# Attention inside a four-block model: a group's maxima turned and their score unit issued ahead of the step's end, score units moved up by one place, query chunks moved

## The reference, cut to what matters

```python
q = (x @ wq_w.T + wq_b).reshape(b, t, H, HD)          # H = 32, HD = 32
k = (x @ wk_w.T + wk_b).reshape(b, t, HKV, HD)        # HKV = 1
v = (x @ wv_w.T + wv_b).reshape(b, t, HKV, HD)
scores = jnp.einsum('bqhd,bkd->bhqk', q, k1) / jnp.sqrt(jnp.float32(HD))
scores = jnp.where(causal, scores, -jnp.inf)
weights = jax.nn.softmax(scores, axis=-1)
attn = jnp.einsum('bhqk,bkd->bqhd', weights, v1)
return attn.reshape(b, t, H * HD) @ wo_w.T + wo_b
```

## Time and profile before

| | |
|---|---|
| median of 3 runs | 2989.56 us (2985.69 to 2994.57) |
| the profiled execution's own time | 2977.39 us |
| its span, first to last instruction | 2975.7 us |
| PE busy | 2750.2 us (92%) |
| DVE, ACT, POOL busy | 1679.5, 1159.2, 948.6 us |
| mean granted TensorE clock | 0.958 |

### The profile page before, as it was taken

One profiled execution on the slowest core, in us unless ns is written; L12 is line 12 of the kernel. 1 busy time (PEld: TensorE's weight loads), 2 busy tenths in 40 slices (PEclk: granted clock), 3 DMA queues, 4 the chain that ended last, 5 costly groups with the idle time before them and its releaser, 6 DMA issues. The chain is left out here.

```text
span 2975.7 us, 41796 instructions
## 1 busy us (share of the span) xinstructions
PE 2750.2 (92%) x15104; PEld 2015.2 (68%) x15104; DVE 1679.5 (56%) x4305; ACT 1159.2 (39%) x2509; POOL 948.6 (32%) x1460
## 2 busy tenths in 40 slices
PE   5888999999999999999999987999999999999988
PEld 3556667667566676676665565777877777878766
DVE  3554464663745646637445346666666666666653
ACT  3664464562644645626445012222222222222220
POOL 2433122221221222212213044444444444444422
PEclk8889999999999999999999888999999999999989
DMA  5755545444536454445455510010101010102011
GB/s 157 197 167 157 167 104 163 124 113 145 129 82 174 109 154 125 113 144 124 94 143 153 172 43 1 4 54 3 55 4 54 5 54 2 56 1 57 2 27 29
DMA packets 103631, 272.29 MB, mean 92 GB/s; under 512 B 12122, under 2 KB 23514, under 8 KB 101122
## 3 DMA queue, kind: packets, MB, share of 16 engines
q1 hardware_dynamic: 102706, 269.55, 33.6%
q10 hardware_dynamic: 720, 0.07, 0.0%
HBM read 168.40 MB, written 50.33 MB: 74 GB/s over the span
## 5 line engine op out<-in xcount | busy, mean ns | idle before, releaser
L664 DVE CUSTOM_DVE_ANT_0 ps_attn<-ps_attn,later_keys 128x512 f32<-128x512 f32 (+3 forms) x1024 | 485.9, 512 | 403.0 <-PE ps_attn L837 400.7
L474 POOL TENSOR_SCALAR_AFFINE_SELECT pt<-pt 128x512 f32<-128x512 f32 x256 | 165.4, 648 | 905.1 <-ACT pt L561 903.9
L561 ACT ACTIVATE pt<-ps_attn 128x512 f32<-128x512 f32 (+1 forms) x704 | 385.9, 560 | 102.1 <-PE ps_attn L865 90.4
L1559 PE MATMUL ps_mixer<-m_w_hi,m_xt_hi 128*128 128x512 f32 x1024 | 421.2, 411 | 1.6 <-DVE m_xt_lo L1341 1.6
L576 ACT ACTIVATE ps_attn<-ps_attn,top 128x512 f32<-128x512 f32 (+1 forms) x512 | 312.6, 611 | 247.1 <-DVE top L664 245.1
L1560 PE MATMUL ps_mixer<-m_w_hi,m_xt_lo 128*128 128x512 f32 x1024 | 406.4, 397 | 0.0
L1561 PE MATMUL ps_mixer<-m_w_lo,m_xt_hi 128*128 128x512 f32 x1024 | 405.8, 396 | 0.0
L865 PE MATMUL ps_attn<-q_stack,k_stack 97*128 97x512 f32 (+3 forms) x1024 | 314.4, 360 | 37.2 <-DMA q_stack<-top_rows 25.7
L837 PE MATMUL ps_attn<-k_stack,q_stack 96*128 96x512 f32 (+3 forms) x1024 | 306.6, 352 | 38.6 <-DMA q_stack<-q_lo 15.0
L1241 ACT CAST m_xt_hi<-ps_mixer 128x512 fp32r<-128x512 f32 x192 | 104.1, 589 | 494.0 <-PE ps_mixer L1554 493.8
L837 PEld LDWEIGHTS ps_attn<-k_stack,q_stack 96*128 96x128 f32 x1024 | 175.5, 195 | 129.1 <-ACT ps_attn L576 72.8
(11 more groups left out here) (216 smaller groups left out, 4937.0 us busy)
## 6 DMA issues: line engine op xcount, KB each, us to landing
xr<-in_a_x SPq DMA_DIRECT2D x64, 512.0 KB, 6.8
q_stack<-q_hi SPq DMA_DIRECT2D x128, 256.0 KB, 5.6
wq_hi<-wq_split SPq DMA_DIRECT2D x56, 512.0 KB, 3.9
wq_lo<-wq_split SPq DMA_DIRECT2D x56, 512.0 KB, 4.6
q_stack<-q_lo SPq DMA_DIRECT2D x64, 256.0 KB, 6.8
wo_hi<-wo_split SPq DMA_DIRECT2D x8, 2048.0 KB, 8.3
wo_lo<-wo_split SPq DMA_DIRECT2D x8, 2048.0 KB, 13.1
x<-xr SPq DMA_DIRECT2D x32, 512.0 KB, 2.8
```

The lines of the kernel that those rows point to most:

```text
L561: nc.scalar.activation(pt[k][:, heads[0]:heads[0] + len(heads), :].rearrange("p j t -> p (j t)"), ps[:, ST0 + n % 2, 0:width * len(heads)] ...
L664: mm = nc.vector.tensor_tensor_reduce(part, part, later_keys[:, T - width:T], 1.0, NO_SCORE, ALU.add, ALU.min, top[:, j * TILES + i:j * TI ...
L1559: nc.tensor.matmul(out, a_hi, b_hi, start=first, stop=False)
```

## The change

Four things are moved; no instruction is added to or taken from the work that a group needs.

1. The turn, `copy_rows` and `shift` of group M+1 come in step M where `turned_early(M + 1)` holds, which is for all groups but the last two of each sequence (groups 6 and 7; those of the last sequence are early too). On PE the turn stands ahead of turned unit 10 of group M, on ACT the copy ahead of `exps` 10, on SP the DMA at the end of step M, ahead of the stores of an output run. Before, all three stood at the start of step M+1.
2. Score units move up: units 2 and 3 behind turned unit 0, and from there unit u+3 behind turned unit u, where unit u+2 stood. `weigh_first` stands behind score unit 1, before it stood ahead of score unit 0.
3. The query chunks of a step with projection were spread as 0 ahead of the turn, 1 and 2 behind score units 0 and 1, then 3, (4, 5), (6, 7) behind turned units 0, 1, 2; now chunk 0 stands behind score unit 0, then (1, 2), (3, 4), (5, 6, 7) behind turned units 0, 1, 2.
4. In step 6 `q_high` moves from u = 2 to u = 4 on ACT, and `q_low` behind `tops` 7 on DVE. In the other steps both stay.

Two waits for PSUM banks (`y_added` in `tops_turned`, `top_rows_done` in `output`) are set one group later to fit.

```diff
--- before.py
+++ after.py
@@ -335,6 +335,9 @@
         def x_banks(b, t):
             return (AV, DEN) if b == 0 and t % 2 else (PROJ, MISC)
 
+        def turned_early(G):
+            return inside(G) and not (G % GROUPS >= GROUPS - 2 and G // GROUPS + 1 < BATCH)
+
         def wq_group(M):
             return M + 3 if M + 3 < GROUPS else None
 
@@ -430,7 +433,7 @@
                     if M == NG:
                         sp.wait_ge(b_done, 2 * NG)
                         early.load(sp)
-                    if inside(M):
+                    if inside(M) and not turned_early(M):
                         shift(M)
                     if M > GROUPS and M % GROUPS == 1 and inside(M):
                         load_wo(M // GROUPS - 1)
@@ -458,6 +461,8 @@
                         store_wo_chunk(c)
                     if (c := wo_chunk(M + 1)) is not None:
                         load_wo_chunk(c)
+                    if turned_early(M + 1):
+                        shift(M + 1)
                     if (run := output_run(M)) is not None:
                         b, r = run
                         store(b, 2 * r)
@@ -623,11 +628,13 @@
                     if M == -1:
                         q_high(1)
                     for u in range(U):
+                        if u == U - 1 and turned_early(M + 1):
+                            copy_rows(M + 1)
                         if inside(M):
                             exps(M, (u,))
                         if inside(M + 1):
                             row_sum(M + 1, u + 2)
-                        if u == 2 and inside(M + 2) and M != -1:
+                        if u == (4 if second is not None else 2) and inside(M + 2) and M != -1:
                             q_high(M + 2)
                         if u == 3 and M == -1:
                             wq_high(act, 2)
@@ -732,10 +739,12 @@
                         normalise(dve, b, t)
                     if inside(M + 1):
                         tops(M + 1, (4, 5))
-                    if inside(M + 2) and M != -1:
+                    if second is None and inside(M + 2) and M != -1:
                         q_low(M + 2)
                     if inside(M + 1):
                         tops(M + 1, (6, 7))
+                    if second is not None and inside(M + 2):
+                        q_low(M + 2)
                     if inside(M - 1):
                         invert(M - 1, 0)
                     if inside(M + 1):
@@ -849,8 +858,8 @@
                         pe.wait_ge(v_done, b + 2)
                     if G:
                         pe.wait_ge(top_rows_done, G)
-                    if b and g in (1, 2):
-                        pe.wait_ge(y_added, Y_TILES * (b - 1) + TILES * g)
+                    if b and g in (2, 3):
+                        pe.wait_ge(y_added, Y_TILES * (b - 1) + TILES * (g - 1))
                     nc.tensor.transpose(ps[:, MISC, 0:P], top[:, :].bitcast(F32), ident_f).then_inc(topt_ready, 1)
 
                 def turned_scores(G, u):
@@ -911,7 +920,7 @@
                         elif t == 0:
                             pe.wait_ge(qlo_done, min(GROUPS * (b + 1) + run + 3, NG))
                         else:
-                            pe.wait_ge(top_rows_done, min(GROUPS * (b + 1) + run + 1, NG))
+                            pe.wait_ge(top_rows_done, min(GROUPS * (b + 1) + run + 2, NG))
                         tok = slice(t * P, (t + 1) * P)
                         for c in range(CH):
                             if run == 0 and t == 0 and c == CH - 1:
@@ -923,30 +932,33 @@
                 for M in STEPS:
                     first, second = coming(M, 5), coming(M, 6)
                     project = second is None and inside(M + 2)
-                    shares = ((0, 1, 2, 3, 4), (5, 6), (7,), (), (), ()) if M == -1 else ((0,), (1,), (2,), (3,), (4, 5), (6, 7))
+                    shares = ((0, 1, 2, 3, 4), (5, 6), (7,), (), (), ()) if M == -1 else ((), (0,), (), (1, 2), (3, 4), (5, 6, 7))
                     if project:
                         q_part(M + 2, shares[0])
-                    if inside(M):
+                    if inside(M) and not turned_early(M):
                         tops_turned(M)
                     if second is not None:
                         transposes(second, 2)
-                    if inside(M - 1):
-                        weigh_first(M - 1)
                     if inside(M + 1):
                         scores(M + 1, 0)
                     if project:
                         q_part(M + 2, shares[1])
                     if inside(M + 1):
                         scores(M + 1, 1)
+                    if inside(M - 1):
+                        weigh_first(M - 1)
                     if project:
                         q_part(M + 2, shares[2])
                     if second is not None:
                         transposes(second, 3)
                     for u in range(U):
+                        if u == U - 1 and turned_early(M + 1):
+                            tops_turned(M + 1)
                         if inside(M):
                             turned_scores(M, u)
-                        if u + 2 < U and inside(M + 1):
-                            scores(M + 1, u + 2)
+                        if inside(M + 1):
+                            for n in ((2, 3), (4,), (5,), (6,), (7,), (8,), (9,), (10,))[u] if u < 8 else ():
+                                scores(M + 1, n)
                         if project and u < 3:
                             q_part(M + 2, shares[u + 3])
                         if second is not None:
```

## The result

| | before | after |
|---|---|---|
| median of 4 runs | 2987.62 us | 3078.01 us (3066.07 to 3083.47) |
| the profiled execution's own time, span | 2977.39, 2975.7 | 3080.04, 3078.3 |
| mean granted TensorE clock | 0.958 | 0.935 |

The changed kernel is slower: ratio 1.0324, 95% interval 1.0296 to 1.0352. The direction is the forecast one, but the step is +90 us where +43 was forecast, and the time lies just outside the range. The fourth run of before, made beside the changed kernel, brings its median from 2989.56 to 2987.62; the quotient of the two medians is 1.0303, inside the interval.

The account below looks back on a forecast made before the run. An ordinary step was taken as bounded by TensorE and DVE at once. Six batches +28, the last +5, the first +5, shift waits -5 and clock +10 made +43 on 2989.56: 3033 us, range 2982 to 3075.

Parts of the forecast that it names:

- A: Ordinary step, from the turn to the last query matmul: grows from 8.30 to 9.66 us.
- B: Ordinary step, from the last query matmul to the next turn: shrinks from 8.28 to 7.93 us, limited by DVE.
- "faster" rival: Ordinary steps: the turn comes as early as TensorE's own work allows, steps about 16 us, total 2945; chance 0.14.
- The stack's landing: Ordinary step: the query stack's DMAs land 9.2 us behind the last query matmul.
- a wait of 0.6: TensorE at score unit 0: reaches it at 8.6 us and waits 0.6 us for the stack, making the period 18.2.
- The table: Forecast times by step M % 8: 39.5 for output runs, 18.2 for ordinary steps, 19.9, 28.6 and 18.4 for steps 5 to 7.
- +4.7 a batch from the chains: Over a batch of eight steps: time grows from 195.8 to 200.5 us.
- the forecast without its clock term: Whole kernel: the forecast growth of +43 us without the 10 us added for the clock.
- The clock, +10 in all: Whole kernel: TensorE idles twice around each turn, for which 10 us were added.
- the clock falls more often: TensorE around early turns: a clock fall in every one of 50 steps, +65 us instead of 10, 3088; chance 0.13.
- every second one: The case of a clock fall in every second step, priced at 3055 us in all.
- Shift waits, -5: TensorE's waits for the shift, 4.5 us in 1400: cured by the earlier copy and shift, counted as -5 us.

Follow-up runs that it names:

- l1: The changed kernel with q_low written behind maxima 7 in every step: 3091.4 us, ratio 1.0386 to the kernel before.
- u3: The changed kernel with the query chunks placed as in the kernel before: 3041.3 us, ratio 1.0223 to the kernel before.
- f4: The changed kernel with four unread matmuls ahead of each early turn, its wait for DVE behind them: 3027.5 us, ratio 1.0183 to the kernel before.
- f2: The changed kernel with two unread matmuls ahead of each early turn, its wait for DVE behind them: 3063.0 us, ratio 1.0289 to the kernel before.
- f7: The kernel before with the early turn alone and seven unread matmuls ahead of each early turn: 3001.6 us, ratio 1.0070 to the kernel before.
- f6: The changed kernel with four unread matmuls ahead of each early turn and two more ahead of score unit 0: 3032.8 us, ratio 1.0198 to the kernel before.
- p1: The kernel before with the early turn, copy and shift alone: 3089.1 us, ratio 1.0393 to the kernel before.
- p3: The kernel before with the query chunks moved back alone: 3087.6 us, ratio 1.0375 to the kernel before.

## Why the prediction was right or wrong

- **A, turn to last query matmul, 9.66:** right, 9.8: 10.49 less 0.66 of stack wait.
- **B, last query matmul to turn, 7.93:** right, 7.81, and maxima 7 at 2.70 as forecast (2.7). But the reason that I gave the "faster" rival, q_low in the way, is wrong: l1 shows that row sum 5 and score unit 7 hold maxima 7.
- **The stack's landing, 9.2, and a wait of 0.6 where a step's score unit 0 needs it:** right, 1251.85 - 1242.53 = 9.32 to the start of score unit 0, a wait of 0.65 to 0.78. That 0.6 less would come out without it is wrong: u3 is free of the wait and has the same 18.31.
- **The table:** 39.38 for 39.5, 18.29 for 18.2. Step 6 fell to 30.1, not 28.6. Alone, part 4 did a little better than I said, 28.9 on average where the sum without the chunk's move gives 29.2. In the whole change a new wait of 2.54 takes its place, that of score unit 4 for row sum 2. Row sum 2 waits 1.03 on ACT for maxima 2; these stand on DVE behind the low part of the transposed tokens, which waits 1.54 for ACT's casts:

```profile
859.64 1.29 DVE L658 TENSOR_TENSOR xn_lo<-ps_attn,xn_hi 128x512 fp32r<-128x512 f32 x2 [1.54 <-ACT xn_hi L545]
861.63 0.66 ACT L581 ACTIVATE ps_attn<-ps_attn,top 128x512 f32<-128x512 f32 x1 [1.03 <-DVE top L671]
862.46 0.44 PE L846 MATMUL ps_attn<-k_stack,q_stack 96*128 96x384 f32 x1 [2.54 <-ACT ps_attn L581]
```

- **+4.7 a batch from the chains:** right in size. f4, whose low time is nearly that of before, has 1013.1 - 984.2 = 28.9 in five batches; less 7 us of low clock at 0.46, 25.7, that is 5.1 a batch. In part that is luck: in f4's two batches whose only fall is that of step 6, step 5 takes 21.1 to 21.2 where I had 19.9, step 7 takes 17.0 where I had 18.4, and the two cancel. Over all of attention, to the last turn, f4 is 1654.8 - 1611.6 = 43.2 longer, where the forecast without its clock term is 33; 12.1 of it arise ahead of the turn of group 16, at the same low time as before (75 us).
- **The clock, +10 in all: the step that failed.** It is the term "PE now idles twice around each turn, and I add 10 for it". In five batches alone 116 - 27 = 89 us more at 1.2 GHz, at 0.33 to 0.46 each, are 29 to 41 of the 66.6 us; f4 against after puts the whole at 42 or more of the 90. The rival "the clock falls more often", to which I gave 0.13, came true on top of the forecast mechanism: 26 falls in those 40 stretches against 8, more than "every second one", which I had priced at 3055, and some of them at 2.5 us (20.79 against 18.3) instead of 1.3. The low clock goes with the idle time ahead of the turn (f2, f4, f7). I had counted the one at score unit 0 alike: filling it as well changed nothing (f6), while taking it away with the turn's gap left open halved the low time (u3). The Trainium skill (TensorE: Matmul & The Clock Gate, Part 1) says that activity frees the clock and idling throttles it; the runs agree.
- **Shift waits, -5:** they went from the list of waits as forecast; no run prices them apart.
- **What the forecast could have seen:** step 28 at 0.94 against step 27 had the price of a fall, and my own B had 1.0 us of idle ahead of each of some 40 turns. What it didn't have was how many of these bring a fall, and I took a number near none. The part-by-part view was missing too: p1 and p3 each cost at least as much as the whole, since each removes, from ahead of the turn, the work that covered DVE's last maxima.

## What to carry to other kernels

Work that stands in a queue where its engine would wait anyway is free. Moving it behind the wait adds its own time on the new side and shortens nothing on the old side, where idle time takes its place, here 0.7 to 1.4 us a step. On TensorE that idle time can cost more than the chain: with 1.40 us in each early step, p1 lost 3.2% by the granted clock and 0.7% by its chain; a stretch at PEclk 1.00 beside one of the same work below 1.00 gives the price, and a few unread matmuls in the gap tell the two costs apart. Try the parts of a bundled change one by one: three of these four raised the time or served to soften another, and one (the step 6 edit, 17 us) was a plain gain that the bundle hid.

## What the runs showed of the hardware

- The clock answers by degrees: gaps ahead of the turn of 1.32, 0.97 and 0.50 us, with the same clean step of 18.3, went with 116, 89 and 34 us at 1.2 GHz. Neither that gap nor PE's idle time in all gives the low time by itself: u3 has the gap of 1.32 and 55 us, and p1, whose clean step idles at the turn alone (1.40), has 195. PE's waits between those turns add up to 98 us in after and 97 in u3, to 66 in f4 and 67 in p1.
- A us at 1.2 GHz cost 0.33 to 0.46 us of time, less than the half that a stretch bound by TensorE alone would lose. That waits take up the rest is likely, but not shown.
- The stack's three transfers share one rate in these kernels. In l1 the last of them was issued 834.00 - 831.18 = 2.8 behind the first, in after 1.25, and it landed 5.2 us behind its own issue where it took 6.7 to 6.9. Counted from the first issue both land after 8.0 to 8.1 us: 768 KB at 96 to 98 GB/s. So the 6.7 that my sum used was set by the transfers ahead of it; issued 1.6 later, the same transfer took 5.2.

```profile
831.18 1.21 SPq L424 DMA_DIRECT2D q_stack<-q_hi  x2
834.00 0.55 SPq L424 DMA_DIRECT2D q_stack<-q_lo  x1
```
